# First and last tile of two large attentions: exponentials and sums by bank, scaling on VectorE, and a later combination of batch 1

## The reference, cut to what matters

```
x = x + tanh(g_xattn[1]) * _L1_xattn_ref(_layernorm(x), ctx, Wq, Wk, Wv, Wo)
...
scores = einsum('bhqd,bhkd->bhqk', q, k)        # 16 heads, 77 keys
attn = softmax(scores / sqrt(Dh))
out = einsum('bhqk,bhkd->bhqd', attn, v)
```

## Time and profile before

| what | value |
|---|---|
| median of 3 runs | 306.43 us (305.58 to 308.19) |
| profiled execution, its time | 304.07 us |
| profiled execution, its span | 302.3 us |
| TensorE busy | 271.6 us, 90% of the span |
| VectorE busy | 204.9 us, 68% |
| ScalarE busy | 151.0 us, 50% |
| GpSimd busy | 121.9 us, 40% |
| mean granted TensorE clock | 0.983 |

### The profile page before, as it was taken

The page is one execution under the profiler, slowest core; times in us unless marked ns, Lnnn a source line. Parts: engine busy times, 40 slices in busy tenths (PEclk is TensorE's granted clock), DMA queues, the critical chain, the costliest instruction groups (busy, mean ns, idle before and its releaser), DMA issues.

```text
span 302.3 us, 5461 instructions
## 1 busy us (share of the span) xinstructions
PE 271.6 (90%) x1930; PEld 197.1 (65%) x1930; DVE 204.9 (68%) x582; ACT 151.0 (50%) x333; POOL 121.9 (40%) x135
## 2 busy tenths in 40 slices
PE   8999887999989998779999979987999778879996
PEld 2578776799989974348888733544667543556475
DVE  2857899022821118999976458889999689988741
ACT  1220785522332366855454578148566745762331
POOL 6364227777756513345354100206653602421100
PEclk9999998999999999799999998999999999999999
DMA  6970407998897132095000100000000000000002
GB/s 173 356 252 1 141 22 249 345 295 236 240 313 256 35 94 64 4 358 194 2 1 2 69 0 2 0 0 0 2 4 0 2 0 0 2 0 3 0 8 64
DMA packets 17912, 28.65 MB, mean 95 GB/s; under 512 B 3632, under 2 KB 10494, under 8 KB 17886
## 3 DMA queue, kind: packets, MB, share of 16 engines
q1 hardware_dynamic: 15972, 25.12, 24.7%
q0 software_dynamic: 1536, 3.02, 3.9%
q10 hardware_dynamic: 378, 0.16, 0.3%
HBM read 25.21 MB, written 3.08 MB: 94 GB/s over the span
## 4 chain that ended last, share of the span: by engine, by line
PE 51%; DVE 24%; ACT 8%; DMA 6%; issue 6%; POOL 2%; SPq 1%; POOLq 0%; DVEq 0%; ACTq 0%
PE bank L1263 6%; PE bank L1326 6%; PE bank L1255 6%; PE bank L1003 4%; DVE pmax L1901 4%; DVE pr L1902 4%; PE bank L1030 4%; DVE psums L1908 3%; PE bank L1309 3%; PE bank L1223 3%; DMA w_router<-in_w_router 2%; DMA yt<-acc,back 2%; ACT pr L840 2%; DMA pr<-lnd,source 2%; PE bank L1548 1%
## 5 line engine op out<-in xcount | busy, mean ns | idle before, releaser
L577 POOL TENSOR_TENSOR rstd<-var,minus_half 128x4 f32<-128x4 f32 x16 | 16.5, 1030 | 70.7 <-DVE var L1597 70.5
L602 POOL TENSOR_TENSOR pr<-pr,psums 128x1232 f32<-128x1232 f32 x12 | 27.0, 2248 | 34.4 <-DVE psums L1910 34.4
L1030 PE MATMUL bank<-onesb,identb 128*128 128x512 bf16 x121 | 32.8, 395 | 0.0
L694 ACT ACTIVATE prT<-bank 128x512 f32<-128x512 f32 (+1 forms) x48 | 22.0, 486 | 20.9 <-PE bank L1003 20.6
L799 ACT ACTIVATE prT<-bank 128x512 f32<-128x512 f32 x23 | 13.7, 598 | 31.6 <-PE bank L1255 31.6
L1901 DVE TENSOR_REDUCE pmax<-bank 128x6 f32<-128x462 f32 (+1 forms) x48 | 26.9, 560 | 3.0 <-PE bank L1313 1.8
L1866 DVE COPY acc<-bank 128x128 f32<-128x128 f32 x23 | 6.7, 291 | 32.0 <-PE bank L1263 24.9
L656 POOL DMA_INDIRECT yt<-acc,back x23 | 22.8, 990 | 11.6 <-DVE acc L1866 7.0
L1003 PE MATMUL bank<-ident,pr 128*128 128x128 f32 (+1 forms) x140 | 21.8, 286 | 5.0 <-ACT prT L697 3.4
L1255 PE MATMUL bank<-prT,experts 128*128 128x128 f32 x184 | 25.1, 281 | 0.5 <-issue 0.5
L1263 PE MATMUL bank<-experts,prT 128*128 128x128 f32 x184 | 24.2, 276 | 0.9 <-DVE acc L1866 0.9
(11 more groups left out here) (356 smaller groups left out, 578.3 us busy)
## 6 DMA issues: line engine op xcount, KB each, us to landing
experts<-in_w SPq DMA_DIRECT2D x23, 512.0 KB, 5.2
experts<-in_w SPq DMA_DIRECT2D x2, 2048.0 KB
lnd<-ln SPq DMA_DIRECT2D x4, 256.0 KB, 2.6
experts<-yt SPq DMA_DIRECT2D x4, 256.0 KB, 3.0
x<-in_x SPq DMA_DIRECT2D x2, 256.0 KB, 3.9
wkv<-in_wk SPq DMA_DIRECT2D x1, 512.0 KB, 6.9
wkv<-in_wv SPq DMA_DIRECT2D x1, 512.0 KB, 6.4
wqT<-in_wqT SPq DMA_DIRECT2D x1, 512.0 KB, 7.0
```

Source lines behind the costliest of these rows:

```text
L602: pool.tensor_tensor(v, v, psums[:, n % 4, 1, :].unsqueeze(2).to_broadcast([P, H, R]), ALU.mult).then_inc(p_ready, 1)
L694: ins = act.activation(dst[:, c0:full, :], bank[:, 0:(full - c0) * P].rearrange("p (c k) -> p c k", k=P), ACT.Copy)
L1030: pe.matmul(bank[:, :].rearrange("p (c k) -> p c k", c=C), identb[:, :], onesb[:, :].unsqueeze(1).to_broadcast([P, C, P]), start=True, sto ...
```

## The change

In both attentions, for tiles 0 and 7: ScalarE makes the exponential by bank (`exps_by_bank`: three instructions of 462, 462 and 308 columns, each as soon as its bank's `less_max` is done); VectorE makes the sums by bank, the reciprocals, and then itself the scaling, in two halves of 8 heads (`probabilities`); TensorE waits for a half (`p_fast`) instead of for GpSimd. Tile 1 gets one exponential and a sum on VectorE, as the others have. VectorE finishes `probabilities(0)` before it begins with tile 1. In L1x, `combine_second` comes one tile later (behind the third `less_max` of tile 2), batch 1's rows are transposed behind all of tile 1's transposes, ScalarE copies them behind all of tile 1's copies, and in n = 1 `weighted(0)` comes first and `scores(4)` behind those transposed rows. GpSimd normalises tiles 1 to 6 only.

```diff
 # bank order, ring TR
-            if n == 1:
+            if n == 1 and layer == "L2x":
                 t.append(("lnT", layer, 1))
             t += [("pT", layer, n, i) for i in range(len(TCH))]
+            if n == 1 and layer == "L1x":
+                t.append(("lnT", layer, 1))
 # ScalarE
-                def exps_and_sums(n):
+                def exps_by_bank(n):
                     act.wait_ge(*rstd_done(layer, n // TB))
                     for i, (h0, h1) in enumerate(HEADS):
+                        v = pr4[n % 4][:, h0 * R:h1 * R]
                         act.wait_ge(*S.freed((layer, n, i)))
-                        for h in range(h0, h1):
-                            v = pr4[n % 4][:, h * R:h * R + R]
-                            ins = act.activation(v, v, ACT.Exp, scale=rstd[:, n:n + 1],
-                                                 accum_out=psums[:, n % 4, 0, h:h + 1])
-                    ins.then_inc(p_exp, 1)
+                        act.activation(v, v, ACT.Exp, scale=rstd[:, n:n + 1]).then_inc(
+                            part_exp if i < len(HEADS) - 1 else p_exp, 1)
...
-                exps(0)
-                exps_and_sums(1)
+                exps_by_bank(0)
+                exps(1)
...
-                    if n == 1:
+                    if n == 1 and layer == "L2x":
                         transposed(layer, 1)
                     for i, (c0, c1) in enumerate(TCH):
                         if i == len(TCH) - 1 and n + 2 < T:
-                            exps(n + 2)
+                            if n + 3 < T:
+                                exps(n + 2)
+                            else:
+                                exps_by_bank(n + 2)
...
+                    if n == 1 and layer == "L1x":
+                        transposed(layer, 1)
 # TensorE
-                    if n == 1:
+                    if n == 1 and layer == "L2x":
                         transpose_rows(layer, 1)
-                    pe.wait_ge(p_ready, T * (layer == "L2x") + n + 1)
+                    if 0 < n < T - 1:
+                        pe.wait_ge(p_ready, (T - 2) * (layer == "L2x") + n)
                     for i, (c0, c1) in enumerate(TCH):
+                        if n in (0, T - 1) and i < 2:
+                            pe.wait_ge(p_fast, 4 * (layer == "L2x") + 2 * (n == T - 1) + i + 1)
...
                         if i == len(TCH) - 1:
-                            if n + 3 == TB:
-                                pe.wait_ge(*(S.freed(("q2", 1)) if layer == "L2x" else lnT_done("L1x", 1)))
-                            if n + 3 < T:
+                            if layer == "L1x" and n + 3 == TB:
+                                weighted(n - 1)
+                            elif n + 3 < T:
+                                if n + 3 == TB:
+                                    pe.wait_ge(*S.freed(("q2", 1)))
                                 scores(n + 3)
                             else:
                                 weighted(n - 1)
                         transpose_chunks(("pT", layer, n, i), pr4[n % 4], c0, c1, ident)
+                    if layer == "L1x" and n + 3 == TB:
+                        transpose_rows(layer, 1)
+                        pe.wait_ge(*lnT_done(layer, 1))
+                        scores(n + 3)
...
-                    if 1 <= n and n + 3 < T:
+                    if 1 <= n and n + 3 < T and not (layer == "L1x" and n + 3 == TB):
                         weighted(n - 1)
 # VectorE
+                def probabilities(n):
+                    rows = pr4[n % 4].rearrange("p (h r) -> p h r", h=H)
+                    parts = len(HEADS) - 1
+                    for i, (h0, h1) in enumerate(HEADS):
+                        if i < parts:
+                            dve.wait_ge(part_exp, parts * (2 * (layer == "L2x") + (n == T - 1)) + i + 1)
+                        else:
+                            dve.wait_ge(p_exp, base + n + 1)
+                        ins = dve.tensor_reduce(psums[:, n % 4, 0, h0:h1], rows[:, h0:h1, :], AX, ALU.add)
+                    step(ins)
+                    step(dve.reciprocal(psums[:, n % 4, 1, :], psums[:, n % 4, 0, :]))
+                    for h in range(0, H, H // 2):
+                        v = rows[:, h:h + H // 2, :]
+                        dve.tensor_tensor(v, v, bc(psums[:, n % 4, 1, h:h + H // 2], R), ALU.mult).then_inc(p_fast, 1)
                 for i in range(len(HEADS)):
                     less_max(0, i)
-                for n in range(T):
-                    early = 1 if n == 0 else 2
-                    if n + 1 < T:
-                        for i in range(early):
-                            less_max(n + 1, i)
+                probabilities(0)
+                for i in range(len(HEADS)):
+                    less_max(1, i)
+                for n in range(1, T - 1):
+                    for i in range(2):
+                        less_max(n + 1, i)
                     sums(n)
-                    if n + 1 < T:
-                        for i in range(early, len(HEADS)):
-                            less_max(n + 1, i)
-                    if layer == "L1x" and n == 0:
+                    for i in range(2, len(HEADS)):
+                        less_max(n + 1, i)
+                    if layer == "L1x" and n == 1:
                         combine_second()
+                probabilities(T - 1)
                 finish(0)
```

More of the change, by code:

```diff
@@ L411, in program @@
         p_exp = sem("p_exp")
+        part_exp = sem("part_exp")
+        p_fast = sem("p_fast")
         p_recip = sem("p_recip")
@@ L596, in add_bias, with normalise @@
                                        ALU.add).then_inc(biased, 1)
-            def normalise(layer, first=0, last=T):
+            def normalise(layer, first, last):
                 for n in range(first, last):
-                    pool.wait_ge(p_recip, T * (layer == "L2x") + n + 1)
+                    pool.wait_ge(p_recip, (T - 2) * (layer == "L2x") + n)
                     v = pr4[n % 4].rearrange("p (h r) -> p h r", h=H)
@@ L660, in _ @@
             pool.tensor_tensor(gy[:, 0, TB:T, :], gy[:, 0, TB:T, :], gy[:, 1, TB:T, :], ALU.add).then_inc(combined, 1)
-            normalise("L1x", 0, 1)
+            normalise("L1x", 1, 2)
             inverse_root("L1x", 1, B)
-            normalise("L1x", 1, T)
+            normalise("L1x", 2, T - 1)
             inverse_root("L1f")
@@ L669, in _ @@
             inverse_root("L2x")
-            normalise("L2x", 0, 2)
+            normalise("L2x", 1, 2)
             add_bias("L2x", bo2, 2)
-            normalise("L2x", 2, T)
+            normalise("L2x", 2, T - 1)
             inverse_root("L2f")
@@ L1906, in sums @@
                     dve.wait_ge(p_exp, base + n + 1)
-                    if n != 1:
-                        step(dve.tensor_reduce(psums[:, n % 4, 0, :], pr4[n % 4].rearrange("p (h r) -> p h r", h=H),
-                                               AX, ALU.add))
+                    step(dve.tensor_reduce(psums[:, n % 4, 0, :], pr4[n % 4].rearrange("p (h r) -> p h r", h=H),
+                                           AX, ALU.add))
                     dve.reciprocal(psums[:, n % 4, 1, :], psums[:, n % 4, 0, :]).then_inc(p_recip, 1)
+                def probabilities(n):
[12 more added lines that the diff above has]
+                        dve.tensor_tensor(v, v, bc(psums[:, n % 4, 1, h:h + H // 2], R), ALU.mult).then_inc(p_fast, 1)
```

## The result

| | before | changed |
|---|---|---|
| median of 4 runs | 306.00 us (305.06 to 308.19) | 316.37 us (313.48 to 318.37) |
| profiled execution | 304.07 us | 317.72 us |
| its span, mean granted clock | 302.3 us, 0.983 | 315.9 us, 0.962 |

The ratio is 1.031, 95% interval 1.025 to 1.038; it leaves out the run of 318.37 us, which counts as a slow one. Forecast were 314.7 us (309.5 to 317.5) and "slower" at 0.82: right in sign and in range, 1.7 us short.

What follows compares the result with a forecast made beforehand. VectorE was taken to bound L1x's start and L2x's steady part, TensorE the rest of L1x. L1x +6.4 and L2x +1.9 gave +8.3 us on 306.43, so 314.7 us, range 309.5 to 317.5.

Steps and rivals of the forecast that it cites:

- What bounds: L1x: VectorE bounds the start, TensorE the rest at 5.40 us a tile; L2x's steady part is VectorE's at 4.91.
- Rival 2: L1x: VectorE's slack takes up its added 2.9 us; total +2.3 us, 308.7 us; chance 0.08.
- VectorE's added work, +2.9: Start of an attention: tile 1's sum, tile 0's halves and bank sums, less a short wait, add 2.9 us (2.7 to 3.2).
- lm(3): The third `less_max` of tile 3; in L1x forecast to end 2.9 us later, at 139.44 us.
- `combine_second` only changes its place, it adds nothing by lm(3): L1x's start: this addition stays ahead of tile 3, so it adds 0 before tile 3's third `less_max` ends.
- rival 4: Both attentions: the scaling halves meet GpSimd, 2.9 us more in each; total +14.1 us, 320.5 us; chance 0.04.
- The order in L1x: L1x: scores(4) waits behind exps(3) and the copy of batch 1's rows, 2.13 us, starting at about 141.8 us.
- Clock in L1x, 1.75 (0 to 2.5): L1x: behind TensorE's 4.0 us wait, 3.5 us at half clock on scores(4) and tile 2 cost 1.75 us.
- Rival 1: Idle stretch costs no clock, +6.5 us, or L2x's last tile also gives back GpSimd's full step, +4.3; chance 0.15.
- L1x's tail, -0.2: End of L1x: a fast tile 7 saves 0.2 us of a 0.26 us wait for GpSimd.
- L2x, +2.5 and -0.6: L2x: scores(4) comes 2.5 us later (2.2 to 2.9); the end saves 0.6 (0 to 2.8); together +1.9.
- Rival 3: L2x's start: tile 1's single exponentials were the last wait, one exponential saves 2.2 us; total -3.0, 303.4 us; chance 0.09.

Runs made afterwards that it cites:

- e3: Changed kernel with unread products in TensorE's idle stretches of both attentions; ratio 1.024 to the kernel before, L1x 59.34 us, L2x 51.28.
- e7: Changed kernel with `combine_second` moved ahead of tile 1's sum; ratio 1.018 to the kernel before, L1x 57.92 us, L2x 51.85.
- e1: Changed kernel with L1x put back in its old order; ratio 1.018 to the kernel before, L1x 58.15 us, L2x 51.26.
- e2: Kernel before with tile 7 alone done by VectorE, table load left in place; ratio 0.996, L1x 52.67 us, L2x 48.70.
- e6: Kernel before with tile 7 alone done by VectorE and L2x's table load behind the attention's last copy; ratio 0.995, L2x 47.87 us.
- e4: Kernel before with tile 1 alone changed: one exponential on ScalarE, its sum on VectorE; ratio 1.016, L1x 55.59 us, L2x 50.32.
- e5: Kernel before with tile 0 alone changed: exponentials and sums by bank, scaling in halves on VectorE; ratio 1.007, L1x 53.84 us, L2x 51.57.
- e8: Kernel before with tile 7 on VectorE, L2x's table load moved, and 7 idle products ahead of scores(2)'s third bank; ratio 0.995, L1x 52.68 us.

## Why the prediction was right, and where it was short

- **What bounds.** Right for L1x. A delay of scores(4) stays: tile to tile is 5.40 us again. Rival 2 (VectorE's slack takes it up) is out. With scores(4) late, VectorE at 4.91 and TensorE at 5.40 are so near that in e3 and e7 the chain ran in VectorE. In L2x, which I had put down to VectorE at 4.91, the chain of the changed kernel runs in TensorE, at 4.84 and 4.87 us a tile: there too the two are near each other.
- **VectorE's added work, +2.9.** The terms held: halves 1.51 together (forecast 1.5), sums by bank 1.54 to 1.58 for three. A single half took 0.80, the dearer of my two values, but its working was wrong: the line through 429 and 626 ns has a start-up of 0.04 us only, which gives 0.75. lm(3) ended 4.16 later from the first score product (24.59 for 20.43); less the 1.22 of the addition that is 2.9.
- **"`combine_second` only changes its place, it adds nothing by lm(3)".** This step failed, by 1.2 us. I had the earlier trace rows with the addition at 0.89 and used it against the halves (rival 4), but did not ask what GpSimd does at the addition's new place. e1, e3 and e7 show it: 0.68 with GpSimd idle (e1, e7), 2.11 under its scaling (e3); e7 is the changed kernel otherwise. The halves never met GpSimd, and rival 4 did not come. The Trainium skill (GPSIMD Engine Reference, Key points) warns of VectorE instructions with two SBUF inputs beside GpSimd; these runs agree, on an instruction other than the one that I tested the rule on.
- **The order in L1x.** exps(3) to the end of the copy of the rows took 2.14 us, forecast 2.13. scores(4) came at 142.9 in old-kernel time, forecast 141.8; the difference is the addition's. e1 puts the order's whole price at 3.2 us.
- **Clock in L1x, 1.75 (0 to 2.5).** Right in kind, short in size: scores(4) lost 2.41 and tile 2's transposes 0.34, 2.75 together, above my bound, as the half level lasted through all of scores(4). What can be had back is 2.0 (e3, and e7 by another way). Rival 1 (no clock) is out for L1x.
- **L1x's tail, -0.2.** Nothing came (e2: +0.07). With these, 6.4 + 1.2 - 0.15 for the restart that was 0.05 and not 0.2, + 1.0 of clock + 0.2 of tail = 8.7, which is what was measured.
- **L2x, +2.5 and -0.6.** Without the clock (e3) scores(4) came 2.54 later and the stage grew by 2.0, forecast 1.9. The clock, which I held hidden (0 to 1), cost 1.25 in the profiled execution: there are two idle stretches, the second right ahead of the queries. In e1, where it fell behind the first, it cost nothing. The tail gave 0.4 (0.5 in e2 and e3); the reason that I gave for its being small, ScalarE's table, holds in part: with the load moved (e6) it gives 1.37, of the 2.8 that GpSimd's step would be worth.
- **Rival 3 (tile 1's single exponentials were the wait).** Out: e4 does just that and is 1.6% slower.

The parts add up once the clock is taken out. Alone they cost L1x 1.24 (e5), 2.99 (e4) and 0.07 (e2), together in the old order 5.55 (e1), which is 1.25 more. What the half level cost tile 1's transposes and scores(4), against the 1.06 and 2.07 of the kernel before, was 2.77 in e1, 1.54 in e4 and nothing in e5. Less that, the parts are 1.24 + 1.45 + 0.07 = 2.76 and the whole is 2.78. How the clock fell in the changed kernel's other three runs was not profiled; that their times follow their mean clocks is all that is known.

## What to carry to other kernels

Before moving a two-input VectorE instruction, look in the trace at what GpSimd does at the new place, not only at what the move frees. Where an engine's step is taken off a path by giving it to the engine that feeds the bound one, count it in full: GpSimd's 2.25 us for tile 0 was hidden, VectorE's 1.5 was not. And price a longer idle stretch of TensorE twice: once as the wait, and once for the work at half level behind it, if that work is on the chain.

## What the hardware showed that I had not expected

- A VectorE addition of 512 columns with two SBUF inputs took 0.68 us with GpSimd idle and 2.11 under GpSimd's two-input scaling. It ended 0.54 us after that did, so in 1.57 us beside it VectorE did only 0.14 us of its work. The old place fits too: in the kernel before, GpSimd's scaling of tile 0 (timeline below) ended at 126.13, 0.35 us into the addition at 125.78, which took 0.89, 0.21 too long, and ended 0.54 us after it as well.

```profile
123.88 2.25 POOL L602 TENSOR_TENSOR pr<-pr,psums 128x1232 f32<-128x1232 f32 x1 [4.15 <-DVE psums L1910]
```

- The same idle stretch need not be followed by the same clock, even in the same program: behind 2.83 us in L2x the changed kernel stayed at 1.00 and fell behind the next stretch of 2.52, while e1 and e7 fell behind the first (2.82 and 2.83). e5 fell behind its own 2.83 (0.57 over the 4 us from 223) and had lost nothing by the queries. Which stretch it is made up to 1.3 us of difference, for what follows the first lies mostly under VectorE's work, and what follows the second on the chain.
- Idle products that held the clock at 1.00 in the changed kernel went with a spread of its runs of 0.6 us instead of 4.9 (four runs each). In the kernel before they did not narrow it: e6 spreads over 1.9 us and e8 over 2.8 (twelve runs each). So the narrowing is not shown to be theirs.
